# The routed experts of a decoder layer's feed-forward part: 22 dense half blocks a group against 15 tiles of scattered rows

## The chip, the cores and the metric

The kernel runs on one core of one Trainium2 chip. Its time is the device's, in microseconds (us), of one execution. Three runs of the kernel before took 638.73 to 642.28 us, median 638.91. One more execution was profiled: its trace spans 636.7 us, and all rows below are of it.

## The reference, cut to what matters

One decoder layer for x of 16 x 128 tokens with 256 channels, in float32: `x` plus a recurrent attention, plus a causal cross-attention of 16 heads over a context, plus a feed-forward part. The change is in the last:

```python
shared = einsum(silu(x @ sw_gate) * (x @ sw_up), sw_down)            # 704 hidden columns, every token
probs = softmax(x @ router_w.T)                                      # E = 8 experts
top_w, top_i = top_k(probs, 2); top_w /= top_w.sum()
h = silu(einsum('th,ehi->eti', x, w_gate)) * einsum('th,ehi->eti', x, w_up)   # I = 176 for each expert
routed = einsum('eth,te->th', einsum('eti,eih->eth', h, w_down), combine)     # combine: top_w at top_i, else 0
out = x + routed + sigmoid(x @ shared_gate_w)[:, None] * shared
```

So of each token's eight experts only two carry a weight.

## The kernel before

**Groups and points.** The 16 sequences are worked in NG = 4 groups of GB = 4, so 512 tokens (GT) a group. A group g passes through four stretches: recurrent attention ("scoring": score products L1153, VectorE's product with the decay L1574, value products L1164, POOL's masked copies of the receptance L579), the norms and projections (points n0 to n5), the cross-attention as a loop over four sequences (points x0a, x0b, x0c to x3c), and the output projection (L1237) with the router (points y0, r0 to r3). At each point the engines also take up work of the feed-forward part of the group before. `POINTS` and `COUNT` (L401 to L406) say how many "ticks" stand at which point, each engine's program is written in that order by hand, and semaphores tie them together; there is no scheduler.

**The feed-forward part** (`ffn_tick` on each engine). All eight experts' 1408 hidden columns and the 704 shared ones are computed for all tokens, in 17 row blocks of 128 (FB) by two halves of 256 tokens (HT), that is 34 half blocks a group (FN; L38): 22 of the experts, 12 shared. Tick n issues on TensorE `gate_up(f, n)` (L1044 to L1046: 12 products of 256 columns; 6 in the last, packed block) and `down(f, n - 2)` (L1084 to L1086: six products into one accumulating bank). Float32 products are done with high and low parts, hence three products for one. Between them: ScalarE's SiLU (L799), VectorE's product with the up half (L1549), POOL's product with the routing weight (L625), ScalarE's high part (L789), POOL's low part (L614). The weights come broadcast over partitions by SP's DMAs (L468) from a DRAM table (`cw_rows`), which `turn_routing` (L1103) and a store of SP fill per group. VectorE adds a finished half into the residual (L1544) and SP stores it.

**The cross-attention loop**, per sequence b: query scores (mask product L1274, scores L1281); VectorE's maximum over them (L1652) and two small steps (L1656, L1660); their transpose (L1286), ScalarE's copy (L898); key scores (L1295, L1300); four exponentials on ScalarE (L907), four causal selects on POOL (L689); the attention product (L1314); ScalarE's and VectorE's steps on the result (L914, L915, L1673 to L1685). ScalarE needs one table for the exponential and another for SiLU; L820 calls the first early, L799 brings the second back.

```python
for b in range(GB):                      # TensorE, groups 1 to 3
    query_scores(b)
    point(g, f"x{b}a")                   # 1 tick of group g-1; x{b}b 1, x{b}c 2
    turn_maxima(b)
    point(g, f"x{b}b")
    key_scores(b)
    point(g, f"x{b}c")
    attend(b)
```

**The router** (L1385, L1395; VectorE L1772 to L1797) finds two masks `r_o1`, `r_o2` and the weights. **The last group's part** has no attention beside it. TensorE issues four gate-up blocks ahead of `turn_routing`, in all AHEAD = 10 ahead of the first down product (L1409 to L1414); ScalarE `silu_last` L805, VectorE `product_last` L1802, POOL `scale_last` L714 and low part L723; then the residual (L1807) and the stores (L512).

## Time and profile before

| what | value |
|---|---|
| timed runs (three) | 638.73 to 642.28 us, median 638.91 |
| span of the profiled execution | 636.7 us |
| TensorE, products | 599.7 us busy, 94% of the span |
| TensorE, weight loads (beside the products) | 483.6 us |
| VectorE | 409.6 us |
| ScalarE | 278.9 us |
| POOL | 342.8 us |
| DMA | 34.08 MB, mean 54 GB/s |

PE is TensorE, PEld its weight loads, DVE VectorE, ACT ScalarE, POOL GpSimd, SP SyncE; L12 is line 12 of the kernel. In the table of stretches, a row gives the window in us from the span's start, its length, for each engine the busy time and in brackets its instructions, the granted TensorE clock (PEclk, 1.00 is full), the DMA engines' busy share and GB/s. In a timeline a row gives start, duration, engine, line, operation, output<-input, shape and count; square brackets at the end are the idle time before it and what released it. In a table of groups a row gives busy time, mean ns of one, and the idle time before them.

### The profile page before, as it was taken

The numbers are of one execution on the slowest core, as the hardware profiler recorded it, in microseconds if no ns is written. First come the engines' busy times: TensorE is split into PE (matmuls) and PEld (weight loads), VectorE is DVE, ScalarE is ACT, GpSimd is POOL, SyncE is SP. The second block draws the span as 40 slices with busy tenths as digits, with TensorE's granted clock in tenths as the row PEclk, the third lists the DMA queues.
The fourth block names the chain that finished last, engine by engine and source line by source line (L and its number), as shares of the span: only waits on it lengthen the run. The fifth ranks groups of instructions, "written<-read, shape, count | busy, mean of one in ns | idle before, by whom it ended". The sixth has DMA issues, their size and how long they took to land.

```text
span 636.7 us, 15520 instructions
## 1 busy us (share of the span) xinstructions
PE 599.7 (94%) x6307; PEld 483.6 (76%) x6307; DVE 409.6 (64%) x841; ACT 278.9 (44%) x637; POOL 342.8 (54%) x462
## 2 busy tenths in 40 slices
PE   7987967979999999999999999999999999999997
PEld 6544545636988889755888889864898888899997
DVE  5997897778744755869644755869762655752221
ACT  4867224232335556342435555251435555343332
POOL 7684145247446667614456666615364666519766
PEclk9999999979999999999999999999999999999999
DMA  8931000020121121011021111002011112014320
GB/s 189 343 104 35 1 1 4 0 68 6 39 67 39 43 60 43 14 34 51 30 80 36 39 52 49 23 17 69 18 51 34 39 44 60 29 38 123 97 55 16
DMA packets 41824, 34.08 MB, mean 54 GB/s; under 512 B 9901, under 2 KB 41206, under 8 KB 41754
## 3 DMA queue, kind: packets, MB, share of 16 engines
q1 hardware_dynamic: 39850, 31.27, 18.2%
q10 hardware_dynamic: 1904, 1.84, 0.9%
q8 instruction: 49, 0.80, 0.5%
q14 instruction: 21, 0.17, 0.1%
HBM read 30.92 MB, written 2.17 MB: 52 GB/s over the span
## 4 chain that ended last, share of the span: by engine, by line
PE 37%; DVE 25%; POOL 13%; issue 9%; ACT 9%; SPq 1%; DMA 1%; POOLq 0%; ACTq 0%; DVEq 0%
DVE A L1574 7%; DVE nm L1652 5%; PE bank L1040 5%; POOL hb L625 3%; PE bank L1237 3%; POOL A L714 3%; PE bank L1044 3%; PE bank L1045 3%; PE bank L1046 3%; PE bank L1084 3%; POOL hT L614 2%; PE bank L1164 2%; POOL hT_last L723 2%; PE bank L1086 2%; PE bank L1085 2%
## 5 line engine op out<-in xcount | busy, mean ns | idle before, releaser
L614 POOL TENSOR_TENSOR hT<-hb,hT 128x256 fp32r<-128x256 f32 (+1 forms) x102 | 78.0, 765 | 72.0 <-ACT hT L789 72.0
L625 POOL TENSOR_TENSOR hb<-hb,cwb 128x256 f32<-128x256 f32 (+1 forms) x102 | 77.0, 755 | 68.6 <-DVE hb L1549 68.5
L1549 DVE TENSOR_TENSOR hb<-hb,bank 128x256 f32<-128x256 f32 (+1 forms) x102 | 42.7, 418 | 101.6 <-ACT hb L799 101.6
L789 ACT ACTIVATE hT<-hb 128x256 fp32r<-128x256 f32 (+1 forms) x102 | 42.4, 416 | 126.0 <-POOL hb L625 125.8
L1044 PE MATMUL bank<-xTf,wGh 128*128 128x256 f32 x272 | 82.9, 305 | 0.0
L1574 DVE TENSOR_TENSOR A<-bank,decay 128x512 f32<-128x512 f32 x128 | 77.4, 682 | 6.0 <-PE bank L1153 5.9
L1045 PE MATMUL bank<-xTf,wGh 128*128 128x256 f32 x272 | 76.7, 282 | 0.0
L1046 PE MATMUL bank<-xTf,wGl 128*128 128x256 f32 x272 | 76.5, 281 | 0.0
L1045 PE MATMUL bank<-xTf,wUh 128*128 128x256 f32 x256 | 72.2, 282 | 0.0
L1046 PE MATMUL bank<-xTf,wUl 128*128 128x256 f32 x256 | 72.1, 282 | 0.0
L1044 PE MATMUL bank<-xTf,wUh 128*128 128x256 f32 x256 | 72.1, 282 | 0.0
L579 POOL TENSOR_TENSOR A<-A,mcol 128x512 f32<-128x512 f32 x32 | 34.2, 1076 | 58.7 <-PE bank L1153 55.9
L1084 PE MATMUL bank<-wDh,hT 128*128 128x256 f32 (+1 forms) x204 | 60.5, 297 | 3.2 <-POOL hT L614 3.0
L1044 PEld LDWEIGHTS bank<-xTf,wGh 128*128 128x128 f32 x272 | 51.3, 189 | 8.3 <-issue 5.8
L1086 PE MATMUL bank<-wDh,hT 128*128 128x256 f32 (+1 forms) x204 | 57.1, 280 | 0.0
L1085 PE MATMUL bank<-wDl,hT 128*128 128x256 f32 (+1 forms) x204 | 57.1, 280 | 0.0
L799 ACT ACTIVATE hb<-bank 128x256 f32<-128x256 f32 (+1 forms) x102 | 38.1, 374 | 39.5 <-PE bank L1046 37.6
L1045 PEld LDWEIGHTS bank<-xTf,wGh 128*128 128x128 f32 x272 | 51.4, 189 | 0.2
L1046 PEld LDWEIGHTS bank<-xTf,wGl 128*128 128x128 f32 x272 | 51.2, 188 | 0.0
L1044 PEld LDWEIGHTS bank<-xTf,wUh 128*128 128x128 f32 x256 | 48.3, 189 | 0.0
L1046 PEld LDWEIGHTS bank<-xTf,wUl 128*128 128x128 f32 x256 | 48.2, 188 | 0.0
L1045 PEld LDWEIGHTS bank<-xTf,wUh 128*128 128x128 f32 x256 | 48.2, 188 | 0.0
(230 smaller groups left out, 1418.3 us busy)
## 6 DMA issues: line engine op xcount, KB each, us to landing
cwb<-cw_rows SPq DMA_DIRECT2D x54, 128.0 KB, 2.9
A<-cw_rows SPq DMA_DIRECT2D x18, 128.0 KB, 4.0
A<-in_x SPq DMA_DIRECT2D x4, 512.0 KB, 4.3
res<-in_x SPq DMA_DIRECT2D x4, 512.0 KB, 4.8
out_x<-res SPq DMA_DIRECT2D x8, 256.0 KB, 2.4
rawG<-in_L_ffn_w_gate SPq DMA_DIRECT2D x2, 704.0 KB, 6.6
rawU<-in_L_ffn_w_up SPq DMA_DIRECT2D x2, 704.0 KB, 6.6
cwb<-cw_rows SPq DMA_DIRECT2D x12, 112.0 KB, 2.6
```

Of the source, the lines that this page charges most:

```text
L614: pool.tensor_tensor(hT[hr, c % 2, 1, :], hb[hr, c % 2, :], hT[hr, c % 2, 0, :].bitcast(F32), ALU.subtract).then_inc(h_lo, 1)
L625: pool.tensor_tensor(hb[hr, c % 2, :], hb[hr, c % 2, :], cwb[hr, c % CWS, :], ALU.mult).then_inc(h_scaled, 1)
L789: act.activation(hT[hidden(n), c % 2, 0, :], hb[hidden(n), c % 2, :], ACT.Copy).then_inc(h_hi, 1)
L799: act.activation(hb[hidden(n), c % 2, :], PS[5 + c % 2][hidden(n), 0:HT], ACT.Silu).then_inc(silu_done, 1)
L1044: mm(out_ap, wh, xh, start=start, stop=False, skip_group_check=skip)
L1045: mm(out_ap, wh, xl, start=False, stop=False, skip_group_check=skip)
L1046: return mm(out_ap, wl, xh, start=False, stop=stop, skip_group_check=skip)
L1084: mm(o, hi[:, t], wDh[hr, j, :], start=(j == 0 and b == 0), stop=False, skip_group_check=True)
L1085: mm(o, hi[:, t], wDl[hr, j, :], start=False, stop=False, skip_group_check=True)
L1086: last = mm(o, lo[:, t], wDh[hr, j, :], start=False, stop=j == FB - 1, skip_group_check=True)
L1549: tt(h, h, up_part(PS[5 + c % 2], n), ALU.mult).then_inc(gu_used, 1)
L1574: tt(att[:, (u % 2) * 4 + i, :].rearrange("p (j t) -> p j t", j=4), PS[SCORE_BANKS[(4 * u + i) % 7]][:, :].rearrange("p (j t) -> p j t", j=4),
```

## The change

**What is computed** stays: the two experts of each token alone instead of all eight. **Routed tiles.** When a group's router has its two masks, VectorE keeps them (`chosen`), TensorE counts with small bfloat16 products how many tokens ahead chose the same expert (`rank_tokens`), and VectorE turns the ranks into a slot for each of the 2 x 512 choices (`place_tokens`, nine small steps on VectorE), with each expert's slots beginning at a multiple of 128. Thus 15 tiles of 128 rows (RT = 2 * 512 / 128 + 7) hold every case. POOL scatters the rows of the normed input to DRAM (`xs_rows`) by eight indirect DMAs a group, one per sequence and choice. For groups 0 to 2 these stand between POOL's masked copies (L668) of the next group from its fifth on; for the last group all eight stand ahead of POOL's ticks. Rows of `xs_rows` that no token fills are zero from one DMA at the start (1.9 MB).

**A tile's work**: SP loads it (128 x 256), TensorE transposes it (`turn_tile`, 2), ScalarE takes the high part (L922), VectorE the low (L1790), TensorE computes gate and up for its expert with the weights addressed by a register (`gate_up_routed`, 6 products of 352 columns, tokens on the output's partitions), ScalarE SiLU (L928), VectorE the product in two pieces, TensorE transposes the hidden rows (`turn_hidden`, 2), high and low parts again (L934, L1796), TensorE `down_routed` (5 products of 256), ScalarE copies the result out (L941), SP stores it to `ys_rows`. Four of a group's last ticks each issue two indirect gathers on POOL; VectorE adds the gathered rows times their weight to the residual (`routed_out`, eight additions). The experts' numbers are loaded into TensorE's registers once a group (`load_experts`).

**Shared blocks** stay as before, but without a routing weight: their product with the broadcast weights on POOL, the DMAs of the weights, their DRAM table and `turn_routing` are gone, and the sigmoid gate is multiplied in with the residual.

**Order**: a group f has 30 ticks instead of 36 (`TICKS`; the points x0a to x3a and r0 have one instead of two, r3 is gone). Its first six shared half blocks (all twelve for the last group: `TAIL_AHEAD`) come before the tiles, whose gate-up products stand at ticks AHEAD + 1 to AHEAD + 15; the rest of the shared ones follow. The down product of a tile is one tick late in groups 0 to 2, two in the last. The last group's four gate-up blocks ahead of the routing are gone; its ranks come there.

```diff
+    SFB = -(-SI // P)
+    FN = 2 * SFB
+    RT = 2 * GT // P + E - 1
+    NI = FN + RT
+    TICKS = NI + 3
+    I1 = I - P
+    I2 = 2 * I1
+    TAIL_AHEAD = FN
...
+        AHEAD = [SFB] * (NG - 1) + [TAIL_AHEAD]
+
...
+            return m if m < AHEAD[f] else m + RT
...
+        def routed_item(f, r):
+            return AHEAD[f] + r
...
+        def down_lag(f):
+
+            return 1 if f + 1 < NG else 2
...
+        COUNT = dict(n0=1, n1=2, n2=2, n3=2, n4=1, n5=1, y0=2, r0=1, r1=1, r2=1)
...
             def ffn_tick(f, n):
-                c = f * FN + n
-                if n < FN:
-                    if c >= CWS:
-                        sp.wait_ge(h_scaled, c - CWS + 1)
-                    for a, b, e in expert_rows(n % FB):
-                        hs = slice((n // FB) * HT, (n // FB + 1) * HT)
-                        sp.dma_start(cwb[a:b, c % CWS, :], cwD[f, e, hs].partition_broadcast(b - a)).then_inc(cwb_in[c % CWS], 16)
-                for half, when in ((0, FB + 8), (1, TICKS - 1)):
-                    if n == when:
-                        sp.wait_ge(x3_ready, f * 2 + half + 1)
-                        bs = slice(f * GB + 2 * half, f * GB + 2 * half + 2)
-                        sp.dma_start(out[bs].rearrange("b t c -> t b c"), res[:, f % 2, 2 * half:2 * half + 2, :]).then_inc(out_done, 16)
...
+                if q == 0:
...
+                pool.indirect_dma_start(out=xsD, out_offset=bass.IndirectOffsetOnAxis(ap=pos[:, k, b:b + 1], axis=0),
+                                        in_=tok2[:, b, :], in_offset=None).then_inc(scattered, 16)
+
+            def gather(f, q):
...
+                        pool.wait_ge(o_part, (f + 2) * 4)
+                pool.indirect_dma_start(out=yg[q], out_offset=None, in_=ysD,
+                                        in_offset=bass.IndirectOffsetOnAxis(ap=pos[:, k, b:b + 1], axis=0)).then_inc(yg_in[b // 2], 16)
 
             def ffn_tick(f, n):
-                if split_late("pool", f + 1, n):
-                    low_part(f, n - 1)
-                if n < FN:
-                    c = f * FN + n
-                    pool.wait_ge(gu_used, c + 1)
-                    pool.wait_ge(cwb_in[c % CWS], cwb_landed(f, n))
-                    hr = hidden(n)
-                    pool.tensor_tensor(hb[hr, c % 2, :], hb[hr, c % 2, :], cwb[hr, c % CWS, :], ALU.mult).then_inc(h_scaled, 1)
+                if high_late(f, n):
+                    low_part(f, shared_at(f, n - 1))
...
+                if n >= TICKS - 4:
+                    gather(f, 2 * (n - TICKS + 4))
+                    gather(f, 2 * (n - TICKS + 4) + 1)
...
+            def tile_high(f, r):
+                act.wait_ge(xt_turned, f * RT + r + 1)
+                act.activation(xTf[:, 0, :, (r % 2) * P:(r % 2 + 1) * P], PS[xt_bank(f, r)][:, 0:KC * P].rearrange("p (k t) -> p k t", k=KC), ACT.Copy).then_inc(xt_hi, 1)
...
+            def ffn_tick(f, n, exp_next=False):
+                if high_late(f, n):
+                    high_part(f, shared_at(f, n - 1))
+                if tile_at(f, n) is not None:
+                    tile_high(f, tile_at(f, n))
+                if down_lag(f) == 1 and routed_at(f, n, 1) is not None:
+                    hidden_high(f, routed_at(f, n, 1))
+                if routed_at(f, n) is not None:
+                    silu_routed(f, routed_at(f, n))
+                elif shared_at(f, n) is not None:
+                    silu_shared(f, shared_at(f, n))
+                if exp_next:
+                    act.activation(spare, mhalf[:, 0:1], ACT.Exp).then_inc(exp_table, 1)
+                if down_lag(f) == 2 and routed_at(f, n, 1) is not None:
+                    hidden_high(f, routed_at(f, n, 1))
+                if routed_at(f, n, down_lag(f)) is not None:
+                    take_out(f, routed_at(f, n, down_lag(f)))
+                if high_now(f, n):
+                    high_part(f, shared_at(f, n))
...
+            def gate_up_routed(f, r, e):
+                c, t = f * NI + routed_item(f, r), slice((r % 2) * P, (r % 2 + 1) * P)
...
+                o = PS[5 + c % 2][:, 0:2 * I].rearrange("p (w n) -> p w n", w=2)
+                for k in range(KC):
+                    ws = bass.ds(e * I, I)
+                    mm(o, xTf[:, 0, k, t], wH[:, :, k, ws], start=k == 0, stop=False, skip_group_check=True)
+                    mm(o, xTf[:, 1, k, t], wH[:, :, k, ws], start=False, stop=False, skip_group_check=True)
+                    last = mm(o, xTf[:, 0, k, t], wL[:, :, k, ws], start=False, stop=k == 1, skip_group_check=True)
+                last.then_inc(gu_ready, 1)
...
+                    pe.wait_ge(r_lo, f * RT + r - 1)
+                h, bank = hb[:, c % 2, :], PS[ht_bank(f, r)]
+                nc.tensor.transpose(bank[:, 0:P], h[:, 0:P], ident[:])
+                nc.tensor.transpose(bank[0:I2, P:2 * P], h[:, P:P + I2], ident[:]).then_inc(ht_turned, 1)
...
+            def down_routed(f, r, e):
+                c = f * NI + routed_item(f, r)
...
+                pe.wait_ge(r_lo, f * RT + r + 1)
...
+                    pe.wait_ge(y_out, f * RT + r)
+                h2, o = hT[:, c % 2], PS[y_bank(f, r)][:, 0:C]
+                mm(o, h2[:, 0, 0:P], wDf[:, bass.ds(e * C + DH * C, C)], start=True, stop=False, skip_group_check=True)
+                mm(o, h2[:, 1, 0:P], wDf[:, bass.ds(e * C + DH * C, C)], start=False, stop=False, skip_group_check=True)
+                mm(o, h2[:, 0, 0:P], wDf[:, bass.ds(e * C + DL * C, C)], start=False, stop=False, skip_group_check=True)
+                mm(o, h2[0:I2, 0, P:2 * P], wDf[0:I2, bass.ds(e * C + DM * C, C)], start=False, stop=False, skip_group_check=True)
+                mm(o, h2[0:I1, 1, P:2 * P], wDf[0:I1, bass.ds(e * C + DM * C, C)], start=False, stop=True,
+                   skip_group_check=True).then_inc(down_done, 1)
...
             def ffn_tick(f, n):
-                if n < FN:
-                    gate_up(f, n)
-                if 2 <= n < FN + 2:
-                    down(f, n - 2)
+                if n == R0[f] - 1:
+                    load_experts(f)
+                if tile_at(f, n) is not None:
+                    turn_tile(f, n)
+                if down_lag(f) == 1 and routed_at(f, n, 1) is not None:
+                    turn_hidden(f, routed_at(f, n, 1))
+                r = routed_at(f, n)
+                if r is not None:
+                    gate_up_routed(f, r, expert_of[f][r])
+                elif shared_at(f, n) is not None:
+                    gate_up(f, shared_at(f, n))
+                if down_lag(f) == 2 and routed_at(f, n, 1) is not None:
+                    turn_hidden(f, routed_at(f, n, 1))
+                r = routed_at(f, n, down_lag(f))
+                if r is not None:
+                    down_routed(f, r, expert_of[f][r])
+                if n >= 2 and shared_at(f, n - 2) is not None:
+                    down(f, shared_at(f, n - 2))
 
...
+            def rank_tokens(g):
+                pe.wait_ge(chosen_made, g + 1)
...
-                if g == NG - 1:
-                    for n in range(4):
-                        gate_up(g, n)
                 if g:
...
                     pe.wait_ge(f_lo[1], len(FW))
-            for n in range(4, AHEAD):
-                gate_up(NG - 1, n)
-            for n in range(FN):
-                if n + AHEAD < FN:
-                    gate_up(NG - 1, n + AHEAD)
-                down(NG - 1, n)
+            for n in range(TICKS):
+                ffn_tick(NG - 1, n)
 
...
                     dve.wait_ge(xTf_hi, g * 2 + k + 1)
                     tt(xTf[:, 1, k, :], PS[k][:, :], xTf[:, 0, k, :].bitcast(F32), ALU.subtract).then_inc(xTf_lo, 1)
                 point(g, "r2")
-                point(g, "r3")
                 if g + 1 < NG:
                     for c in range(4 if g else 6, 8):
                         mixed_input(g + 1, c)
+                if g:
+                    routed_out(g - 1, 0)
+                    routed_out(g - 1, 1)
 
                 steps = [0]
```

The three places at which the order of instructions bears on the end are these. First ScalarE, in group 2's cross-attention, third sequence, from the copy of the maxima to the result's first step. In the kernel before (`hb` holds hidden rows, `hT` their high parts, `nmT` the maxima, `bank` is PSUM):

```order
L898 ACTIVATE nmT<-bank 128x128
L789 ACTIVATE hT<-hb 128x256
L799 ACTIVATE hb<-bank 128x256
L820 ACT_TABLE_LOAD
L820 ACTIVATE S<-mhalf 128x1
L789 ACTIVATE hT<-hb 128x256
L907 ACTIVATE A<-bank 128x512 x4
L799 ACT_TABLE_LOAD
L799 ACTIVATE hb<-bank 128x256
L789 ACTIVATE hT<-hb 128x256
L799 ACTIVATE hb<-bank 128x256
L914 ACTIVATE S<-bank,xcol 128x256
```

In the changed kernel, the same place (`xTf` is the tile's transposed input, L941 the result's copy):

```order
L1059 ACTIVATE nmT<-bank 128x128
L922 ACTIVATE xTf<-bank 128x2x128
L934 ACTIVATE hT<-bank 128x256
L928 ACTIVATE hb<-bank 128x176
L955 ACT_TABLE_LOAD
L955 ACTIVATE S<-mhalf 128x1
L941 ACTIVATE A<-bank 128x256
L1068 ACTIVATE A<-bank 128x512 x4
L922 ACTIVATE xTf<-bank 128x2x128
L934 ACTIVATE hT<-bank 128x256
L928 ACT_TABLE_LOAD
L928 ACTIVATE hb<-bank 128x176
```

Two copies of the tile's tick (L922, L934) now stand between the exponentials and the SiLU that reloads the table, and a copy out (L941) ahead of the exponentials. Second TensorE at the hand-over to the last group, from the transpose of the router's logits on. Before (twelve products of a first block, of which the gate's stand here, then three more blocks, then `turn_routing`):

```order
L1395 MATMUL bank<-ident,S 128x128
L1044 MATMUL bank<-xTf,wGh 128x256
L1045 MATMUL bank<-xTf,wGh 128x256
L1046 MATMUL bank<-xTf,wGl 128x256
...
L1103 MATMUL bank<-ident,S 9x128 x4
```

After:

```order
L1631 MATMUL bank<-ident,S 128x128
L1341 MATMUL bank<-chosen,before_tok 128x32
L1343 MATMUL bank<-chosen,onec 128x24
L1343 MATMUL bank<-chosen,onec 128x16
L1343 MATMUL bank<-chosen,onec 128x8
L1345 MATMUL bank<-chosen,onec 128x8 x4
L1191 MATMUL bank<-xTf,wH 128x256
L1192 MATMUL bank<-xTf,wH 128x256
```

The products of the ranks, which need VectorE's masks, have moved ahead of every gate-up block. Third POOL from the end of group 3's points to the end of the program, in the changed kernel (`pos` holds the slots, L712 is the low part of a shared block); before, this place holds only L714 and L723 in turn:

```order
L734 DMA A<-ys_rows,pos 128x256 x4
L724 DMA xs_rows<-A,pos 1920x256 x8
L712 TENSOR_TENSOR hT<-hb,hT 128x256 x5
L712 TENSOR_TENSOR hT<-hb,hT 64x256
L712 TENSOR_TENSOR hT<-hb,hT 128x256 x5
L712 TENSOR_TENSOR hT<-hb,hT 64x256
L734 DMA A<-ys_rows,pos 128x256 x3
L734 DMA rk<-ys_rows,pos 128x256
L734 DMA A<-ys_rows,pos 128x256 x4
```

Eight scatters stand ahead of the first low part of the last group, and eight gathers behind the last.

## Rows read from the trace of the kernel before

**Rows 1.** The page's first line.

```profile
span 636.7 us, 15520 instructions
```

**Rows 2.** Stretches: scoring, norms, four passes, routing (group 2); tail; start of group 1.

```profile
281.60:303.50 21.90, 20.42 (x346) 11.94 (x345) 19.70 (x33) 4.96 (x17) 8.58 (x8) 1.00 0.19 50
303.50:331.60 28.10, 27.64 (x216) 25.10 (x212) 17.56 (x46) 10.57 (x26) 15.08 (x20) 1.00 0.20 60
331.60:396.20 64.60, 63.77 (x768) 56.20 (x767) 36.20 (x63) 36.25 (x79) 38.75 (x57) 1.00 0.17 43
396.20:428.60 32.40, 32.18 (x200) 23.84 (x200) 26.08 (x64) 13.13 (x27) 13.97 (x16) 1.00 0.07 23
577.00:633.40 56.40, 56.05 (x467) 55.24 (x465) 10.81 (x25) 18.88 (x55) 44.23 (x63) 1.00 0.27 67
134.00:140.00 6.00, 6.00 (x49) 2.91 (x48) 4.01 (x7) 1.30 (x4) 2.27 (x2) 0.50 0.34 62
```

**Rows 3.** TensorE's timeline in group 2's second pass of the cross-attention.

```profile
347.40 1.04 PE L1274 MATMUL bank<-maskS,identb 128*128 128x512 bf16 x4
348.37 1.15 PE L1281 MATMUL bank<-A 32*128 32x256 f32 x16
...
356.13 1.11 PE L1300 MATMUL bank<-A 32*128 32x128 f32 x32
...
361.85 1.08 PE L1314 MATMUL bank<-A 128*32 128x128 f32 x32
```

**Rows 4.** TensorE's timeline: routing weights of group 0, neighbouring products, transposes, first tail block.

```profile
133.19 1.01 PE L1103 MATMUL bank<-ident,S 128*9 128x128 f32 x4 [3.50 <-DVE S L1797]
...
328.85 0.40 PE L1256 MATMUL bank<-xT1h,wQh 128*128 128x512 f32 x1
329.08 0.39 PE L1257 MATMUL bank<-xT1h,wUh 128*128 128x512 f32 x1
...
394.13 1.03 PE L1005 MATMUL bank<-ident,A 128*128 128x128 f32 x8
...
560.33 0.36 PE L1044 MATMUL bank<-xTf,wGh 128*128 128x256 f32 x1
```

**Rows 5.** VectorE's timeline: group 2's second pass, a router step, the last addition.

```profile
349.76 2.28 DVE L1652 TENSOR_REDUCE nm<-bank 128x16 f32<-128x2048 f32 x1
...
352.31 0.23 DVE L1660 TENSOR_TENSOR nm<-nm 128x64 bf16<-128x64 f32 x1
352.45 0.41 DVE L1549 TENSOR_TENSOR hb<-hb,bank 128x256 f32<-128x256 f32 x1
...
359.03 2.62 DVE L1685 TENSOR_TENSOR A<-A,S 128x256 f32<-128x256 f32 x1
...
563.43 0.19 DVE L1780 TENSOR_TENSOR S<-S 128x32 f32<-128x32 f32 x1
...
633.41 0.69 DVE L1807 TENSOR_TENSOR res<-bank,res 128x512 f32<-128x512 f32 x1 [7.66 <-PE bank L1086]
```

**Rows 6.** ScalarE's timeline in group 2's second pass of the cross-attention.

```profile
358.12 2.02 ACT L907 ACTIVATE A<-bank 128x512 f32<-128x512 f32 x4
360.16 1.28 ACT L799 ACT_TABLE_LOAD   x1
```

**Rows 7.** POOL's timeline: the selects of that pass, the last norm's power.

```profile
358.98 2.39 POOL L689 TENSOR_SCALAR_AFFINE_SELECT A<-A 128x512 f32<-128x512 f32 x4
...
551.29 1.01 POOL L557 TENSOR_TENSOR rstd<-ve,mhalf 128x4 f32<-128x4 f32 x1 [1.80 <-DVE ve L1436]
```

**Rows 8.** Groups by line and shape on POOL.

```profile
L579 POOL TENSOR_TENSOR A<-A,mcol 128x512 f32<-128x512 f32 x32 | 34.2, 1076 | 58.7 <-PE bank L1153 55.9 <-PE bank L1005 2.7
...
L668 POOL TENSOR_TENSOR res<-res,boB 128x1024 f32<-128x1024 f32 x4 | 9.5, 2365 | 0.0
```

**Rows 9.** DMA issue of SP, and the page's DMA issues (KB each, us to landing).

```profile
L473 SPq DMA_DIRECT2D out_x<-res x6: 388/411/428, 233.2 to 561.1; - x6
...
cwb<-cw_rows SPq DMA_DIRECT2D x54, 128.0 KB, 2.9
```

674 lines of the change are left out of this document (435 added, 239 removed).

## The prediction

> **What bounds the kernel now.** I read the stretches first [rows 2]. The profiled execution spans 636.7 us [rows 1]; the shortest to longest timed runs are 638.73 to 642.28 us and their median, 638.91 us, is 2.2 us above that span. I make the sum on the span and add those 2.2 us. Groups 1 to 3 each pass four stretches, and group 2's stand in [rows 2]. In the scoring stretch (281.6 to 303.5) VectorE is busy 19.7 of 21.9 us. In the three others TensorE is busy 27.64 of 28.10, 63.77 of 64.60 and 32.18 of 32.40 us, since the previous group's feed-forward blocks fill each wait of attention. Behind group 3 comes a tail of nothing but such blocks, 56.05 of 56.40 us busy. So TensorE's work bounds the kernel almost everywhere, and less of it pays only where no chain of waits comes up beneath.
>
> **What TensorE saves.** In the tail, where nothing but products of 256 columns runs, 467 of them fill 56.05 us, 0.12 us each [rows 2]. Two neighbouring ones of 512 columns start 0.23 us apart, and eight transposes take 1.03 us with the last one's latency, 0.12 us each [rows 4]. A dense block of 18 products is 2.2 us. A routed tile has 6 products of 352 columns (0.16 us each by interpolation, 0.97 in all), 5 of 256 (0.6) and 4 transposes (0.48): 2.05 us. 22 dense half blocks a group (47.5 us) become 15 tiles (31 us). That is 16.5 us a group, 66 in all, if nothing else held the engine. I don't take this gain, for the following reasons.
>
> **The four attention loops, the largest term.** Now one loop pass takes 64.6 / 4 = 16.15 us [rows 2]. I lay the new order of each engine along the durations. Time 0 is where the query scores have been issued, which itself takes 2.04 us (347.40 to 349.52, less the overlap with what follows [rows 3]).
> - Tick a: TensorE transposes the next tile and the last hidden rows and runs gate and up: 1.5. The down product waits for VectorE's low parts, and these are queued behind the maximum, 2.28 us and two small steps, to 2.8 (349.76 to 352.54 [rows 5]). Two subtractions follow, 0.34 to 0.42 each (one product of this size: 0.41 [rows 5]): 3.6. Down ends at 4.2.
> - Tick b: transposes, gate and up to 5.7; ScalarE copies 0.7, VectorE subtracts 0.7, down from 6.2 to 6.8. Key scores 1.3 (1.11 us and the short products ahead of them [rows 3]): 8.1.
> - Tick c: ScalarE is now in its four exponentials, 2.02 us [rows 6], to 10.2; behind them two copies, 0.7, the table load for SiLU, 1.28 [rows 6], and SiLU 0.3: 12.5. VectorE's two products end at 13.0. Down of this tick is at 12.9.
> - Second c tick: the hidden rows' transposes need 13.0: 13.4. ScalarE 14.1, VectorE 14.6, down 15.2, attention product 1.08 [rows 3] 16.2, next query scores 2.04: 18.3.
> The dense order survived the same exponentials because its down product is two ticks late and its three copies lie between; the tile's is one tick late, and TensorE stands idle 2.1 us in tick a and 2.7 us in the first c. Its own work in a pass is only 12.7 us. Three passes give 18.3, the last, where three of four ticks have no tile's gate product, 15.7: 70.6 against 64.6, **+6.0 a group, +18**. POOL's selects (2.39 us [rows 7]) and VectorE's stretched product beside them (2.62 us [rows 5]) end at about 11.4 and hide under 12.5.
>
> **Other parts.** Stretch with the norms (303.5 to 331.6): three ticks there get lighter by some 1.5 us, but the one-tick wait in n5 costs about 2.4 us and stands behind the copies of the attention input, and the experts' register load sits in TensorE's queue: +2 a group, **+6**. Scoring stretch, VectorE-bound: nine small steps of place_tokens at 0.22 us each (0.19 us for a step of the router [rows 5], and the way to the next) are +2.1, and six scatters between POOL's masked copies another +0.4: **+7.5** over three groups. Routing stretch: eight additions of gathered rows, 3.3 us, go ahead of the router, and one dense tick less goes from before it; VectorE's chain gets 0.3 us longer: **+1**. Group 0 to 1: TensorE waits 3.50 us for the routing weights [rows 4] and then has half the clock, 0.50 from 134 to 140 us [rows 2], the 1.2 GHz level. The new wait is on the mask, some steps earlier: **-2**. Removed work of POOL and the small broadcasts of weights (66 issues and 128 KB each at most) hide under TensorE: 0. The 1.9 MB of zeros is written during scoring of group 0, which needs no transfer: 0.
>
> **The tail** (before: from 560.3 [rows 4] to the end, 76.4 us). In the same clock times:
> - Gathers 3 to 8 leave POOL behind the norm's power, 552.3 [rows 7], at 1.04 us each with two low parts between, and the last lands 2.9 us later [rows 9]: 563. VectorE adds, then routes: the mask is made at 567.6. In the old order four gate-up blocks ran there; in the new one the ranks come first, so TensorE idles 7.3 us. Ranks 568.3.
> - Three gate-up blocks, most at the lower clock, to 576. The slots are known at 571.0; eight scatters stand on POOL ahead of the first low part: 571.1 + 8 x 1.04 = 579.4, low part 0.75, first down product 580.3.
> - Its 0.7 us, nine ticks of 2.2 us, and half the clock again for 6.8 us (3.4 lost): 604.2. Two mixed ticks, 607.9. Fourteen tile ticks at 2.2 (2.05 of TensorE and some register work): 638.7. The last tile's chain and copy: 641.8.
> - Store 2.5 (like the last one); eight gathers 8.3, which wait for every store; landing 2.9; four additions 1.7; last store 2.6 (from 634.10 to the span's end now [rows 5, 1]): 659.8. **+23.**
>
> Sum: 18 + 6 + 7.5 + 1 - 2 + 23 = +53.5; 636.7 + 53.5 + 2.2 = **692 us**.
>
> **Costs that no row shows.** An indirect transfer's time on POOL: from below SP's issue of a plain one, 0.39 to 0.43 us [rows 9], from above a wide operation of POOL, 2.37 us for 128 x 1024 [rows 8]. I take 1.04 to 1.08, that of its operation of half this width [rows 8], which lies between: POOL has to make 128 addresses each time, more than SP's engine does and less than it computes in the widest. At the lower end the tail is 11 us shorter (681); at the upper end scatters and gathers add 21 us to the tail and, six a group ahead of the masked copies, some 21 us more in scoring (734). The register operations of a tile, seven on TensorE's sequencer: 0 where they run ahead of the products, 0.4 us each tile where not; in the loops idle time takes them, in the tail 15 x 0.4 = +6. Register loads, four: 0 to 2 us each, I have 0.5.
>
> For the landing of a gathered or scattered transfer I use the plain read of 128 KB, 2.9 us [rows 9]. The Trainium skill, "DMA: Bandwidth & Descriptors", section on the anatomy of one DMA, gives POOL's path a fixed 2.0 us and 436 GB/s beside it, 2.3 us here; the sum would then be 691. No run here shows such a transfer yet. The same page's section on latency states a floor of about 600 ns for a tensor load into registers; four of them would be 2.4 us, and the sum the same within 1 us.
>
> **Rivals.**
> - *TensorE stays the bound in the loops* (the opposite sign): if VectorE's and ScalarE's queues let the tile's low parts through in time, a pass is 12.7 us instead of 16.15, -12 a group, -36 in all. With the rest as above: -36 + 6 + 7.5 + 1 - 2 + 23 = -0.5, and with the norm stretch unhurt and the cheap issue (-6 - 11) it is -17.5: 621 to 638, taken at 630. It decides as soon as a pass falls under 14.5 us. For it speaks that TensorE is busy 98% now; against it that maximum, exponentials and table load are fixed in order ahead of the tile's copies. 0.08.
> - *Dear indirect transfers*: 2.37 us each, 734 us. Nothing in the trace is against it but the small row count. 0.15.
> - *Cheap ones*: 681. 0.15.
> - *The clock falls inside the loops*: after 3.5 us of idle it was at half [rows 4, 2]. The new stretches are 2.1 and 2.7 us, and no row has such ones. If it falls in each pass, TensorE's share of the chain, some 6 us at full clock, grows by half, +3 x 12 = +36: 728. 0.09.
> - Gains and losses cancel within 1%: 0.04. My forecast: 0.49.
>
> About 1% is what a measurement of this kernel can tell from no change. Faster has the first rival's 0.08, same 0.04, slower the rest, 0.88. The range leaves out the first rival and the upper half of the dear one. Downward it takes in the cheap issue with passes 2 us shorter than my 18.3, 681 - 24 = 657; upward it ends at 728: 657 to 728.
>
> **What would show it.** Right: in the profile after, loop passes of about 18 us with TensorE idle before the down product, released by VectorE, and before the hidden transposes; TensorE busy below 85% of the span; a gap of some 7 us before the ranks and one before the first down product of the tail, both with the lower clock behind them; some 18 us between the last product and the end. Wrong: passes under 16 us, eight indirect transfers in under 5 us, or a tail without the two gaps.

## The result, and the profile after

The changed kernel takes 756.83 us in the median of four runs (752.14 to 758.54), the kernel before 640.6 us in four runs beside it (638.73 to 643.61): a ratio of 1.180, with a 95% interval of 1.173 to 1.186. It is 18% slower. I had forecast slower, at 692 us in a range up to 728, so the direction held and the size did not.

The page of the changed kernel, its span, TensorE's busy time and the row of the granted clock in 40 slices:

```profile
span 756.8 us, 14812 instructions
...
PE 613.3 (81%) x5639; PEld 456.8 (60%) x5639; DVE 467.6 (62%) x1061; ACT 303.9 (40%) x698; POOL 247.3 (33%) x314
...
PEclk9999999898988979999997999999998999869995
```

The span has grown from 636.7 [rows 1] to 756.8 us, and TensorE is busy 81% of it instead of 94%. The clock row has ten slices under 9, the page of before one. Windows of the changed kernel in the columns of [rows 2]: from group 1's logits to the first score product of group 2, from there to group 2's cross-attention, its four passes, the output projection and router, and the tail.

```profile
314.80:327.50 12.70, 9.26 (x36) 5.31 (x34) 9.12 (x30) 4.23 (x6) 0.95 (x1) 0.87 0.34 95
327.50:381.60 54.10, 48.10 (x536) 34.63 (x533) 41.07 (x96) 16.14 (x44) 23.06 (x24) 1.00 0.12 37
381.60:464.60 83.00, 67.80 (x655) 53.36 (x654) 41.86 (x100) 43.20 (x98) 12.05 (x20) 0.88 0.14 45
464.60:488.80 24.20, 21.99 (x136) 15.92 (x133) 18.54 (x36) 6.97 (x15) 14.99 (x15) 0.93 0.15 44
654.70:756.80 102.10, 65.53 (x438) 59.43 (x438) 36.70 (x120) 32.61 (x87) 26.22 (x30) 0.82 0.24 74
```

The four passes took 64.60 us [rows 2] and now take 83.0, with the granted clock at 0.88; the tail has 102.1 us at 0.82. To see where the 120 us come from, I cut both traces at the same instructions of TensorE: the first query scores of each group, the last attention product and the transpose of the router's logits.

| stretch | before, us | after, us | measured | forecast |
|---|---|---|---|---|
| group 0, to its logits | 126.6 | 138.5 | +11.9 | 0 |
| logits of group 0 to the loop of group 1 | 58.0 | 68.0 | +10.0 | +2.5 |
| the loops of groups 1, 2, 3 | 64.4, 64.5, 62.4 | 84.1, 83.0, 82.2 | +58.0 | +18 |
| loop to logits, three groups | 68.5 | 65.2 | -3.3 | +1 |
| logits to loop, groups 2 and 3 | 58.0, 57.9 | 66.8, 66.8 | +17.7 | +9 |
| tail, from the last logits | 76.4 | 102.1 | +25.6 | +23 |

They sum to +119.9 against 120.1 of the spans. The tail is the only large term that came out as forecast. The loops stand first: TensorE's timeline in group 2's second pass (start, length, engine, line, operation; in square brackets the idle time before it and what ended it). L1525 is query scores, L1298 the first product of a tile's down, L1544 key scores, L1559 the attention product.

```profile
404.33 1.15 PE L1525 MATMUL bank<-A 32*128 32x256 f32 x16
...
409.21 0.58 PE L1298 MATMUL bank<-wD,hT 128*128 x1 [2.18 <-DVE hT L1796]
...
415.47 1.31 PE L1544 MATMUL bank<-A 32*128 32x128 f32 x32
...
420.08 0.38 PE L1298 MATMUL bank<-wD,hT 128*128 x1 [1.75 <-DVE hT L1796]
...
424.04 1.08 PE L1559 MATMUL bank<-A 128*32 128x128 f32 x32
...
426.02 1.15 PE L1525 MATMUL bank<-A 32*128 32x256 f32 x16
```

The two waits that I laid out by hand are there: 2.18 us ahead of the down product of tick a (forecast 2.1) and 1.75 ahead of that of the first tick c (forecast 2.7), both ended by VectorE's low part of the hidden rows. The pass, from L1525 to L1525, is 21.7 us and not 18.3. What the clock did in it:

```profile
408.00:412.00 4.00, 2.79 (x11) 2.34 (x12) 1.39 (x6) 0.93 (x3) 0.00 (x0) 0.63 0.00 0
412.00:416.00 4.00, 4.00 (x40) 3.55 (x42) 2.69 (x5) 2.47 (x6) 0.00 (x0) 0.51 0.21 66
416.00:420.00 4.00, 2.33 (x38) 1.92 (x34) 1.89 (x6) 3.17 (x7) 2.40 (x4) 1.00 0.20 66
```

From 409 us, behind the first wait, it is at half (0.51 in the second window: the 1.2 GHz level), so the ticks a and b and the key scores run slow; at 416 it is at full again. In each of the four passes of this loop the clock is at half once or twice, for 3.4 to 6.8 us. That was the rival to which I gave 0.09. In the view of all waits of TensorE (total us, times, longest) that down product leads. Behind it come the tail's first down product, the transposes of normed rows and the ranks:

```profile
PE bank L1298 <- DVE hT L1796: 43.5, 24, 2.2
PE bank L1232 <- POOL hT L712: 11.7, 6, 7.6
PE bank L1152 <- DVE A L1681: 10.3, 7, 2.3
PE bank L1341 <- DVE chosen L2088: 9.2, 2, 8.9
```

### The profile page after: what moved, and what is told of

Its sections match the earlier page's. It is cut to its first block, busy times and chain, and to the rows that moved or that the text cites. A ratio compares the mean times of both kernels' runs of the same rounds, so it can differ in the third digit from the quotient of the medians.

```text
span 756.8 us, 14812 instructions
## 1 busy us (share of the span) xinstructions
PE 613.3 (81%) x5639; PEld 456.8 (60%) x5639; DVE 467.6 (62%) x1061; ACT 303.9 (40%) x698; POOL 247.3 (33%) x314
## 4 chain that ended last, share of the span: by engine, by line
PE 51%; DVE 27%; ACT 6%; issue 5%; POOL 5%; DMA 1%; POOLq 0%; DVEq 0%
DVE A L1875 6%; DVE nm L1957 5%; PE bank L1187 3%; PE bank L1191 3%; PE bank L1302 2%; PE bank L1406 2%; PE bank L1270 2%; PE bank L1193 2%; PE bank L1192 2%; PE bank L1395 2%; PE bank L1544 2%; PE bank L1272 2%; PE bank L1271 2%; PE bank L1479 2%; PE bank L1525 2%
## 5 line engine op out<-in xcount | busy, mean ns | idle before, releaser
L1298 PE MATMUL bank<-wD,hT 128*128 x60 | 23.6, 394 | 44.5 <-DVE hT L1796 43.5
L1790 DVE TENSOR_TENSOR xTf<-bank,xTf 128x256 fp32r<-128x256 f32 x60 | 25.3, 422 | 50.2 <-ACT xTf L922 50.2
L1191 PE MATMUL bank<-xTf,wH 128*128 128x256 f32 x176 | 56.0, 318 | 0.4 <-ACT A L941 0.4
L712 POOL TENSOR_TENSOR hT<-hb,hT 128x256 fp32r<-128x256 f32 (+1 forms) x48 | 35.1, 733 | 61.8 <-ACT hT L911 61.7
L1187 PE MATMUL bank<-A,wA 128*128 128x512 f32 x96 | 49.2, 656 | 7.5 <-DVE A L1730 6.9
L1193 PE MATMUL bank<-xTf,wL 128*128 128x256 f32 x176 | 52.6, 299 | 0.0
L1192 PE MATMUL bank<-xTf,wH 128*128 128x256 f32 x176 | 52.6, 299 | 0.0
L1395 PE MATMUL bank<-rbdV,A 32*128 32x512 f32 x256 | 45.5, 677 | 8.3 <-DVE A L1875 4.8
L1957 DVE TENSOR_REDUCE nm<-bank 128x16 f32<-128x2048 f32 x16 | 36.7, 2291 | 22.1 <-PE bank L1525 21.8
L668 POOL TENSOR_TENSOR rbdV<-A,mcol 128x512 f32<-128x512 f32 x32 | 35.1, 1104 | 46.1 <-PE bank L1395 45.8
L1270 PE MATMUL bank<-wH,xTf 128*128 x120 | 48.7, 406 | 0.4 <-DVE xTf L1790 0.3
L941 ACT ACTIVATE A<-bank 128x256 f32<-128x256 f32 x60 | 22.9, 381 | 56.8 <-PE bank L1302 55.9
L1298 PEld LDWEIGHTS bank<-wD,hT 128*128 128x128 f32 x60 | 13.8, 230 | 52.8 <-issue 52.8
L734 POOL DMA_INDIRECT A<-ys_rows,pos x28 | 28.2, 1007 | 46.9 <-DMA ys_rows<-A 39.9
L1272 PE MATMUL bank<-wL,xTf 128*128 x120 | 43.0, 359 | 0.0
L1271 PE MATMUL bank<-wH,xTf 128*128 x120 | 42.8, 356 | 0.0
L1406 PE MATMUL bank<-A 128*32 128x128 f32 x1024 | 36.6, 286 | 7.3 <-DVE A L1875 7.3
```

Of the source, the lines that this page charges most:

```text
L1187: last = mm(bank[:, :], wA[:, i, k, m * P:(m + 1) * P], xm[:, c % 4, :], start=k == 0, stop=k == 1)
L1191: mm(out_ap, wh, xh, start=start, stop=False, skip_group_check=skip)
L1192: mm(out_ap, wh, xl, start=False, stop=False, skip_group_check=skip)
L1193: return mm(out_ap, wl, xh, start=False, stop=stop, skip_group_check=skip)
L1270: mm(o, xTf[:, 0, k, t], wH[:, :, k, ws], start=k == 0, stop=False, skip_group_check=True)
L1271: mm(o, xTf[:, 1, k, t], wH[:, :, k, ws], start=False, stop=False, skip_group_check=True)
```

## The experiments

Each is an edit of the changed kernel; "after" without more is its profiled execution of 756.8 us, and its timed runs span 752 to 759 us. Times of the experiments are medians of two runs. Two runs of one kernel lay up to 10 us apart (b2c1), so differences of a few us are read from the traces and not from the times.

**Is it the clock, in the loops?** `fill_loops` puts idle work in the two waits of a pass:

```diff
+            def fill(f, n, r):
+                for _ in range(n):
+                    mm(PS[y_bank(f, r)][:, 0:4 * P], identb[:], identb[:].unsqueeze(1).to_broadcast([P, 4, P]), start=True, stop=True, skip_group_check=True)
...
+                fill(f, FILL.get(n, 0) if f + 1 < NG and routed_at(f, n, 1) is not None else 0, routed_at(f, n, 1))
                 r = routed_at(f, n, down_lag(f))
```

> Kernel after, with 8 and 7 bfloat16 products of 512 columns (some 1.9 and 1.7 us) put on TensorE in the two stretches of each loop pass in which it waits for VectorE's low parts (2.2 and 1.8 us in the trace of after), in tick a and in the first tick c. They write into a free bank and nothing reads them. Theory 1 (the passes are 20 to 21.7 us instead of the 18.3 of my chain because the clock falls to half behind these waits): the granted clock in the loops goes from 0.86 to 0.88 to nearly 1.00, a pass is 18 to 18.5 us, the three loops 26 to 34 us shorter in all, 725 us. Theory 2 (the chain itself is longer than I laid it, by the tile's register operations or the slower products): the passes stay at 20 to 21.7 us or grow by the filler's own time, 757 to 770 us.

It took 737.93 us (737.28 to 738.57). Its window of group 2's four passes, and its row of waits for the down product:

```profile
370.30:446.10 75.80, 71.93 (x708) 50.08 (x707) 42.80 (x100) 42.65 (x98) 12.59 (x20) 1.00 0.15 49
```

```profile
PE bank L1298 <- DVE hT L1806: 8.9, 24, 0.8
```

The clock is 1.00, and the waits fell from 43.5 to 8.9 us in all because the filler stands in them. All 24 waits are still there, so the filler held nothing up. The first three passes of a loop are 19.3 to 19.5 us instead of 20.5 to 22.0, the last is 16.9 to 17.9 instead of 18.2 to 20.3. The three loops are 226.5 us instead of 249.3. So 23 us of the loops' +58 is the clock, which this edit gives back although it adds work to the engine. The rest, +35 at full clock, is the chain of waits: 19.3 us a pass where I had 18.3. Both theories had a part, and the run fell short of the 26 to 34 us of the first.

**Is it the down product one tick late?** `lag2` gives groups 0 to 2 the lag of two ticks that the last group has, and exchanges the banks of the results for it:

```diff
-            return 1 if f + 1 < NG else 2
+            return 2
...
-            return 5 + (f * NI + routed_item(f, r)) % 2 if f + 1 < NG else 0
+            return 5 + (f * NI + routed_item(f, r) + 1) % 2 if f + 1 < NG else 0
```

(The waits for a bank to be read in gate_up, gate_up_routed and down_routed move with it.)

> Kernel after with the down product of a routed tile two ticks behind its gate-up product in groups 0 to 2 too (its result goes to the other of two banks, waits moved with it). Theory 1 (the loops are long because the down product, one tick late, stands behind low parts that VectorE makes after the maximum, and the hidden transposes behind a SiLU that comes after the exponentials; the clock falls in these waits): both waits of TensorE, 2.2 and 1.8 us a pass, go or shrink to under 1 us, by my sum a pass is 16.4 us against 19.3 with the clock held and 20.8 in after, and the clock stays near 1.00: 4 x 4.4 x 3 = 50 us less, 700 to 715 us. Theory 2 (the work of VectorE and ScalarE in a fixed order bounds the pass, however late the down product is): passes of 19 us or more, 735 to 757 us.

It took 713.89 us (713.68 to 714.10), 43 us less, with nothing added or removed on any engine. Its window of group 2's passes, and TensorE's waits in the second one (L1532 transposes the maxima, L1257 the next tile, L1270 is gate and up):

```profile
362.20:433.70 71.50, 61.10 (x660) 47.89 (x659) 43.11 (x100) 42.71 (x99) 12.17 (x20) 0.98 0.15 47
```

```profile
386.35 0.23 PE L1532 MATMUL bank<-identb,nm 128*128 128x128 bf16 x1 [0.38 <-DVE nm L1967]
...
394.47 0.41 PE L1257 MATMUL bank<-ident,A 128*128 128x128 f32 x2 [1.28 <-DVE xTf L1792]
395.37 0.43 PE L1270 MATMUL bank<-wH,xTf 128*128 x1 [0.49 <-DVE hb L1814]
```

The clock is 0.98, the loops are 70.0, 71.5 and 70.6 us, and in them the wait for the down product is gone. What is late next are the maximum (0.38), a tile's low part behind the reciprocal on VectorE (1.28) and its product behind the table load (0.49). This pass is 17.3 us, as most are; my walk gave 16.4. This one number, the lag, carries 37 of the loops' 58 us, the clock's part among them. Still the loops stay 21 us above the kernel before.

**Where the ticks stand.** `b2c1` lays one tick of a pass from c to b; `best2`, below, from c to a.

```diff
-            for p, k in (("a", 1), ("b", 1), ("c", 2)):
+            for p, k in (("a", 1), ("b", 2), ("c", 1)):
```

> Kernel after with the four ticks of a pass laid 1 at a, 2 at b, 1 at c instead of 1, 1, 2. Theory 1 (the wait in the first tick c is for ScalarE's copies queued behind the four exponentials and the table load, and two ticks at c make it come twice in the chain): with one tick there the tile's copies stand less in the way, one of the two waits goes or shrinks, a pass 0.8 us shorter at the same clock by my sum (17.5 for 18.3), and more if the clock then falls once a pass instead of twice: 730 to 747 us. Theory 2 (the passes are bound by the number of tile chains, each of high part, low part and product, wherever they stand): no change, 750 to 760 us.

It took 761.61 us (756.69 to 766.53), not faster. Both waits for VectorE's low part stayed as they were:

```profile
PE bank L1298 <- DVE hT L1796: 43.4, 24, 2.2
```

Moving a tick from c to b moved neither wait. Theory 2 held for this move, with the down product one tick late.

**The hand-over to groups 2 and 3.** VectorE's eight additions of gathered rows stand ahead of the router's steps and of the bias addition (L1730) that frees a bank. TensorE in the changed kernel, with L1187 a projection and L1395 the first score product:

```profile
318.40 1.88 PE L1187 MATMUL bank<-A,wA 128*128 128x512 f32 x4
...
323.71 3.67 PE L1187 MATMUL bank<-A,wA 128*128 128x512 f32 x4 [3.44 <-DVE A L1730]
...
327.49 3.02 PE L1395 MATMUL bank<-rbdV,A 32*128 32x512 f32 x16
```

`adds_late` moves the second four of them behind:

```diff
                 if g:
                     routed_out(g - 1, 0)
-                    routed_out(g - 1, 1)
...
                     take_v(g + 1)
+                if g:
+                    routed_out(g - 1, 1)
```

> Kernel after with the second four of the eight additions of gathered rows put behind the router's steps and the addition of the values' bias on VectorE (the first four must stay, their rows share memory with the router's scratch). Theory 1 (the additions delay the bias addition that frees the bank TensorE waits for, 3.4 us idle at the hand-over of groups 2 and 3): that wait falls by 1.8 us to 1.6, the hand-over by 1.8 to 3 us each, 751 us. Theory 2 (the hand-over is set by the router's steps or by the ranks): under 1 us in all.

```profile
318.92 1.98 PE L1187 MATMUL bank<-A,wA 128*128 128x512 f32 x4 [1.73 <-DVE A L1730]
...
321.02 3.02 PE L1395 MATMUL bank<-rbdV,A 32*128 32x512 f32 x16
```

The wait is 1.73 us instead of 3.44, and the projection behind it takes 1.98 us instead of 3.67: the granted clock behind the wait was 0.55 (323.7 to 327.5 us in after) and is 1.00 here. From logits to score product is 9.3 us (after 12.7, before 7.9). It took 749.73 us (748.27 to 751.18). Four additions, 1.7 us of VectorE, were worth 3.4 us each time: the wait, and as much again in clock.

**VectorE beside POOL.** Two operations of VectorE in the changed kernel take far longer than their like: four normalisations in group 0 (1.38 us for four of the same shape before) and an integer step in group 1 (0.23 us in group 0 and before). VectorE's rows, then POOL's at the same time (L754 splits the down weights, L787 adds a bias, L792 is two memsets):

```profile
125.86 6.08 DVE L1681 TENSOR_SCALAR A<-res,mv,rstd 128x256 f32<-128x256 f32 x4 [0.25 <-POOL rstd L646]
...
173.42 3.23 DVE L1900 TENSOR_SCALAR A<-A 128x128 int32<-128x128 int32 x1
```

```profile
125.79 3.99 POOL L754 TENSOR_TENSOR wD<-rawD,wD 128x512 fp32r<-128x512 f32 x4
...
168.32 4.98 POOL L754 TENSOR_TENSOR wD<-rawD,wD 128x512 fp32r<-128x512 f32 x4 [1.73 <-ACT wD L973]
173.27 2.37 POOL L787 TENSOR_TENSOR res<-res,boB 128x1024 f32<-128x1024 f32 x1
175.59 0.98 POOL L792 MEMSET A<- 128x512 f32 x2
```

The splits of group 1 end at 173.3 us, before the integer step begins. What runs beside it is the bias addition and the memsets, which stand behind the splits on POOL and came late by them. `splits_g1` moves these last four splits behind POOL's masks in point n1, `splits_late` those of group 0 behind the two masked copies of the receptance.

```diff
-                if g == 1:
-                    for n in range(S_PIECES, len(DOWN_PIECES)):
-                        split_down(n)
...
                 point(g, "n1")
+                if g == 1:
+                    for n in range(S_PIECES, len(DOWN_PIECES)):
+                        split_down(n)
```

> Kernel after with the last four splits of the down weights on POOL in group 1 moved behind its masks for the attention values, some 5 us later. Theory 1 (an integer tensor_scalar of VectorE in the variance's square root took 3.2 us instead of 0.2 because these splits and the bias addition run on POOL beside it): it takes under 1.5 us, TensorE's 3.1 us wait for the normalised values shrinks by 1 to 3 us, 753 to 755 us. Theory 2 (it waited for something else): still 3.2 us.

> Kernel after with POOL's splits of the down weights in group 0 moved behind the two masked copies for group 1, away from VectorE's normalisation. Theory 1 (four tensor_scalar operations of VectorE took 6.1 us instead of 1.4 because POOL's splits ran beside them): they take 1.4 again, group 0's routing 4 to 5 us shorter, 752 us. Theory 2 (VectorE waited for something else, a bank or a DMA): still 6 us.

In `splits_g1` the integer step, between the same neighbours:

```profile
168.61 0.23 DVE L1900 TENSOR_SCALAR A<-A 128x128 int32<-128x128 int32 x1
```

So 3.23 us became 0.23 once POOL was free, as theory 1 had it, and the run took 753.59 us (752.58 to 754.61). In `splits_late` the four normalisations still took 4.7 us instead of 6.1, since now the masked copies and then the splits ran beside them. The edit did not leave VectorE alone, so it decides between neither theory. Group 0's output projection and routing were 2.5 us shorter (18.0 us, after 20.5, before 14.6), but the run was not: it took 755.72 us (755.06 to 756.39). The Trainium skill, "SBUF — State Buffer", section on who interferes with whom, says that a VectorE operation in a two-port mode and a GpSimd operation share one pair of ports as an exclusive lock, and the later one blocks until the other ends. The trace agrees, though no row names the mode: taken one by one, the four normalisations last 1.35, 1.35, 0.81 and 2.80 us, each begins 0.07 to 0.11 us after a POOL operation has begun, and each ends 0.15 us after a POOL operation has ended. The last one outlasts three of them. The integer step ends 0.08 us after POOL's second memset.

**The tail.** TensorE from the last logits: the ranks (L1341) and the first down product (L1232). Then POOL: the eighth scatter, the first low parts, the first two final gathers. Then the groups of scatters (L724) and gathers (L734) on POOL, and the gathers' row in the view of the DMAs, us from issue to landing last.

```profile
654.71 0.42 PE L1631 MATMUL bank<-ident,S 128*128 128x128 f32 x1 [0.40 <-ACT S L1114]
664.08 0.21 PE L1341 MATMUL bank<-chosen,before_tok 128*128 128x32 bf16 x1 [8.94 <-DVE chosen L2088]
...
678.33 0.55 PE L1232 MATMUL bank<-wD,hT 128*128 128x256 f32 x1 [7.63 <-POOL hT L712]
```

```profile
676.45 0.97 POOL L724 DMA_INDIRECT xs_rows<-A,pos  x1 [0.30 <-issue]
677.45 1.41 POOL L712 TENSOR_TENSOR hT<-hb,hT 128x256 fp32r<-128x256 f32 x2
...
740.49 0.98 POOL L734 DMA_INDIRECT A<-ys_rows,pos  x1 [39.88 <-DMA ys_rows<-A]
741.78 0.96 POOL L734 DMA_INDIRECT A<-ys_rows,pos  x1 [0.31 <-issue]
```

```profile
L724 POOL DMA_INDIRECT xs_rows<-A,pos x32 | 31.9, 996 | 20.8 <-DVE pos L1856 13.5 <-issue 7.3
...
L734 POOL DMA_INDIRECT A<-ys_rows,pos x28 | 28.2, 1007 | 46.9 <-DMA ys_rows<-A 39.9 <-issue 7.0
```

```profile
A<-ys_rows,pos POOLq DMA_INDIRECT x28, 2.8
```

Both gaps that I forecast are there, 8.94 us (forecast 7.3) and 7.63. An indirect transfer takes POOL 1.0 us and 0.3 to the next, so 1.27 each, 0.2 above my middle value of 1.04 to 1.08. A gather's rows landed 2.8 us after issue, near the 2.9 us of a plain read [rows 9]. The fixed time and the rate that the Trainium skill gives for one DMA of POOL ("DMA: Bandwidth & Descriptors", section on the anatomy of one DMA) make an estimate of 2.3, which the row does not bear out. `spread` puts the scatters in POOL's ticks 3 to 6:

```diff
-            for q in range(2 * GB):
-                scatter(NG - 1, q)
             for n in range(TICKS):
+                if 3 <= n < 7:
+                    scatter(NG - 1, 2 * (n - 3))
+                    scatter(NG - 1, 2 * (n - 3) + 1)
```

> Kernel after with the last group's eight scatters two by two in POOL's ticks 3 to 6, behind the first low parts, instead of all ahead of them. Theory 1 (TensorE's 7.6 us wait ahead of the tail's first down product is the eight scatters, 10 us on POOL): the wait goes nearly whole and with it the half clock behind it; the first tile is needed some 15 us later, so the scatters are hidden there: 7 to 10 us less, 747 to 750 us. Theory 2 (the tiles' arrival moves by as much, since the scatters land later): a new wait ahead of the first tile, 0 to 3 us less.

```profile
677.80 0.39 PE L1233 MATMUL bank<-wD,hT 128*128 128x256 f32 x1 [1.46 <-POOL hT L712]
...
684.20 0.38 PE L1233 MATMUL bank<-wD,hT 64*128 64x256 f32 x1 [1.82 <-POOL hT L712]
```

The wait of 7.63 us ahead of the first down product is gone, and no new one came ahead of the first tile. But two others came, 1.46 us ahead of the fourth block's down product and 1.82 ahead of the sixth's (the rows above), since these low parts now stand behind scatters on POOL. So the tail is only 4.1 us shorter (98.0 us, and 751.07 us for the run), under the 7 to 10 expected. `tailfill` puts idle work into the tail's two waits, 32 products ahead of the ranks and 30 ahead of the first down product. The first edit:

```diff
             def rank_tokens(g):
+                if g + 1 == NG:
+                    for _ in range(32):
+                        mm(PS[4][:, :], identb[:], identb[:].unsqueeze(1).to_broadcast([P, 4, P]), start=True, stop=True)
```

> Kernel after with 32 bfloat16 products of 512 columns on TensorE in its wait ahead of the last group's ranks (8.9 us) and 30 in that ahead of the first down product (7.6 us), into a free bank, read by nothing. Theory 1 (the clock is at half behind each wait, some 3.4 to 4 us, half of that lost each time): granted clock of the tail up from 0.82, 3 to 5 us less, 752 us. Theory 2 (what follows the first wait is hidden by the second, which ends with POOL's work): only the second fall costs, 1 to 2 us.

```profile
649.70:751.70 102.00, 78.76 (x500) 63.79 (x500) 36.72 (x120) 32.47 (x87) 26.44 (x30) 0.89 0.23 74
```

The clock of the tail rose from 0.82 to 0.89, yet the stretch is 102.0 us as before. The rise stands in the wait ahead of the ranks and in the three blocks behind them, and there, unlike in the loops, half clock is hidden, since these blocks end in a wait for POOL. Behind the second wait the clock was at half again, 3.4 us here and 3.8 in after, although 6.65 us of idle work stood in it (TensorE idled the last 1.96). What that second fall costs this run does not show. It took 753.19 us (752.88 to 753.50).

**A tile's own cost on TensorE.** `fixed` takes the expert's number of a tile as tile modulo 8 instead of from a register.

```diff
-                    ws = bass.ds(e * I, I)
+                    ws = slice(e * I, (e + 1) * I)
...
-                    down_routed(f, r, expert_of[f][r])
+                    down_routed(f, r, r % E)
```

> Kernel after with the number of a tile's expert fixed (tile number modulo 8) instead of read from a register: the experts' choice is left out, all instructions and sizes of the products stay, without address registers. A tile's tick in the last group takes 2.35 us on TensorE without a wait, where I had 2.05 to 2.2. Theory 1 (the register operations stand between the products): the tick falls to about 2.05 us, 4 us less in the tail, and each tick of the loops gains as much, 735 to 745 us. Theory 2 (they run ahead of the products, and the two down products with 96 and 48 rows and the change of shape cost the 0.3 us): still 2.35 us, time unchanged within 3 us.

Two tiles' transposes one tick apart in the tail, in `fixed` and in after:

```profile
709.92 0.44 PE L1257 MATMUL bank<-ident,A 128*128 128x128 f32 x2
...
712.26 0.44 PE L1257 MATMUL bank<-ident,A 128*128 128x128 f32 x2
```

```profile
713.65 0.44 PE L1257 MATMUL bank<-ident,A 128*128 128x128 f32 x2
...
716.00 0.44 PE L1257 MATMUL bank<-ident,A 128*128 128x128 f32 x2
```

It is 2.34 us without a register and 2.35 with one. This kernel leaves out the router's choice of expert; the instructions and their sizes stay. The run took 751.56 us (750.86 to 752.26). In the tail the registers cost TensorE nothing; the 0.3 us above my 2.05 are in the first product behind each pair of transposes (0.25 and 0.20 us to the next, not 0.16 and 0.12) and in the two down products of 96 and 48 rows (0.2 and 0.3 us, not 0.12). The 5 us of the whole run lie in the loops (242.7 us against 249.3). Runs that change nothing there spread as well: group 1's loop took 84.1 us in after, 82.6 in adds_late, 80.9 in tailfill and 79.6 here. Whether the registers have a part in that stays open.

**Together.** `best1` is lag2, adds_late, splits_late, spread and two gate-up blocks of the last group ahead of its ranks. `best2` adds splits_g1 and lays a pass's ticks 2, 1, 1. `best3` is best1 with splits_g1 and 18 idle products ahead of the last ranks.

> lag2, adds_late, splits_late and spread together, and the last group's first two gate-up blocks put ahead of its ranks. If these are separate terms of the 120 us they add: 50 + 7 + 1 + 8 + 4 = 70 us less than after, 685 us. If one hides another (the clock's part above all), 700 us. In neither case below the kernel before.

> best1 with the splits moved as in splits_g1 and the four ticks of a pass laid 2 at a, 1 at b, 1 at c. In lag2 TensorE still waits 0.4 to 0.8 us for the maximum and 1.3 + 0.5 us in the second tick c, for VectorE's low part and product behind the reciprocal and the table load. Theory 1 (these waits are a matter of where the ticks lie): with one tick behind the exponentials a pass is 16.0 to 16.5 us instead of 17.3, 682 us. Theory 2 (VectorE's maximum comes later by what the second tick a puts ahead of it, and the pass does not shorten): 690 to 695 us.

> best1 with the splits moved as in splits_g1 and 18 bfloat16 products of 512 columns in TensorE's wait ahead of the last group's ranks (5.0 us in best1). Theory 1 (the clock is at half behind that wait): 2 us from the clock, 1 to 3 from the splits, 690 us. Theory 2: the tail's first down product waits for POOL anyway, so only the splits' part, 693 us.

They took 695.77 us (695.72 to 695.83), 683.89 (682.82 to 684.96) and 696.55 (695.54 to 697.56). The single gains add to 43 + 7 + 1 + 6 us, and best1, with the two early blocks, has 61. In best2 the passes of group 2, and its tail:

```profile
352.70:419.90 67.20, 59.29 (x661) 46.70 (x660) 41.84 (x99) 41.87 (x99) 12.24 (x20) 1.00 0.16 50
589.40:683.20 93.80, 65.08 (x438) 59.08 (x438) 36.63 (x120) 32.50 (x87) 26.46 (x30) 0.85 0.26 81
```

Its loop is 67.2 us, 2.6 above [rows 2]; TensorE is busy 59.3 us of it, 4.5 less than the dense kernel, and waits for the rest. The three loops take 201.4 us, against 212.5 in best1. best3, with the same splits moved and the old order, has 215.5, so the 11 us come from the order 2, 1, 1. That order with the down product one tick late was not run. The tail of best2 is 93.8 us against 76.4. It is the fastest version of this study, a ratio of 1.069 (1.061 to 1.076), and still slower than the kernel before. best3 came out above both of its expectations: its tail is 93.1 us against 92.6 in best1, so idle work ahead of the last ranks returned nothing, and what it gained at the hand-over to group 1 it lost in that group's loop (73 us against 70).

## Why the prediction was right in sign and wrong in size

- **What bounds the kernel, and why less work does not pay.** Right. TensorE was busy 613.3 us after and 599.7 before, half clock included, but 81% of the span. The term that decided was the one I named, a down product one tick late behind maximum and exponentials; lag2 shows it.
- **What TensorE saves, 66 us in all, and 12.7 us of its own work in a pass.** Both too favourable, though the sum used neither. A tile costs TensorE 2.35 us and not 2.05. In the loop of best2, at full clock, it is busy 59.3 / 4 = 14.8 us a pass. In the whole of best2 it is busy 574.8 us, some of it at half clock, 25 less than before where I had reckoned 66. So a part of the gain that I set aside was never there.
- **The loops, +6.0 a group.** This step failed, and it is most of the miss: +19.3 a group. Of the 13.3 above the forecast, 7.6 are the clock (fill_loops) and 5.7 the chain. The chain was mis-sized by 1.0 us in each of the first three passes, and by some 2 in the last. A tile's down takes 0.97 us at full clock and not 0.6; three of them stand on my chain, which fits the 1.0 us, but no run changed it alone.
- **The clock as a rival on its own.** I put waits of 2.1 and 2.7 us in every pass and then let them run at full clock, because no row showed such a wait. The only row that I had, 3.5 us of wait and half clock behind it [rows 4, 2], should have been part of the forecast itself for a chain that waits twice in each of twelve passes. That this rival's +54 us for the loops lies near the +58 measured is luck: it had 36 us of clock and 18 of chain, and the runs show 23 and 35.
- **Routing, +1.** Wrong for the hand-over to groups 2 and 3: +4.8 each. I counted VectorE's chain but not the bank that its bias addition frees, nor the half clock behind that wait. adds_late gives back 3.4.
- **Scoring and norms, +2.5 and +2 a group.** Right where nothing else came in: from first score product to loop, 54.1 us against 50.05 in group 2.
- **Group 0 and the hand-over to group 1, 0 and -2.** Wrong, +11.9 and +7.5 above. VectorE's operations beside POOL's moved splits took 4.7 us more in group 0, and the integer step and the one ahead of it 3.7 us more in group 1, and the clock fell behind these waits too. The prediction never asked what VectorE does while POOL splits. That makes 5.9 us of group 0, from the output projection on, but splits_late gave back only 2.5 of them. The other 6.0 us, ahead of the output projection (it begins at 118.0 us, before at 112.1), were not tested and their cause is open. Runs that change nothing there had it begin at 115.0 to 119.5 us.
- **The tail, +23.** Right, +25.6, with both gaps. The tile's tick is 2.35 and not 2.2, and each indirect transfer 1.27 with the way to the next. That a tile's registers might cost 0.4 us, and its loads 0.5, stood on no row: fixed shows none of it in a tile's tick, and the loads by themselves no run shows.
- **The rival of the opposite sign** needed a pass under 14.5 us. Even best2 has 16.3 to 17.2, and TensorE's own 14.8 us there are above it too, so with this work of TensorE's own it could hardly have come even without a wait.

Of the range: it left out the case that came, in which a longer chain, the clock behind its waits and the losses of group 0 and of the hand-overs all add up.

## What to carry to other kernels

Fewer instructions on the busiest engine pay only if its queue never waits: lay each hand-over between engines at least as many ticks late as the longest operation in the other engine's fixed order asks, before counting the saving. Where a forecast puts a wait in every pass of a loop, price the half clock behind it in the forecast and not beside it; and where work moves on POOL, look which VectorE operations then run beside it.

## What the runs showed of the hardware

- With waits of TensorE of 2.2 and 1.8 us in a pass of some 21 us, the granted clock fell to half in each pass of group 2, for 3.4 to 6.8 us. In lag2, where the longest wait of a loop was 1.8 us and the others at most 1.4, it was 0.98 over four passes.
- Idle products kept the clock at 1.00 and shortened three loops by 23 us; in the tail the same raised it from 0.82 to 0.89 and shortened nothing.
- A float32 tensor_scalar of VectorE (128 x 256) took 0.8 to 2.8 us beside POOL's operations and 0.41 alone (before), an integer one (128 x 128) 3.2 and 0.23. Each ended 0.08 to 0.15 us after an operation of POOL.
- Products addressed by a register took TensorE no longer than those with a fixed address, where it had no waits: 2.35 and 2.34 us a tile.
- An indirect transfer of 128 rows of 1 KB took POOL 1.0 us and 0.27 to 0.3 to the next (32 scatters, 28 gathers), against 0.39 to 0.43 us for SP's issue of a plain one [rows 9].
